# Routing rounds, list scatters and distances between dependent steps in a one-core scan and mixture-of-experts kernel

## What is computed

```python
x = x + layernorm(attn(layernorm(x)))        # x: (4, 1024, 256) f32
x = x + layernorm(ffn(layernorm(x)))

# attn: a state space scan, 16 states for each of 256 channels
xc, z = split(x @ W_in.T)
xs = silu(conv3(xc, conv_w))
dt, B, C = softplus(...), ..., (...) @ W_C.T  # all from xs @ W_x.T
s[t] = exp(-exp(A_log) * dt[t]) * s[t-1] + B[t] * dt[t] * xs[t]
out = (C * s.sum(states) + D * xs) @ W_out.T * silu(z)

# ffn: 8 experts, the best two of each token, and a shared expert
w, sel = top_k(softmax(x @ gate_w.T), 2)      # w made to sum to 1
out = sum_k w_k * (gelu(x @ W1[sel_k] + b1) @ W2[sel_k] + b2)
out = out + gelu(x @ sW1 + sb1) @ sW2 + sb2   # hidden size 1024
```

## Time and profile before

| | us |
|---|---|
| median of 3 runs (lowest, highest) | 1270.08 (1268.75, 1271.2) |
| profiled execution, device time | 1270.0 |
| its span in the trace | 1268.1 |
| TensorE (PE) busy | 1046.6 |
| VectorE (DVE) busy | 711.1 |
| POOL busy | 650.6 |
| ScalarE (ACT) busy | 618.7 |

### The profile page before, as it was taken

The page is one execution under the profiler, slowest core; times in us unless marked ns, Lnnn a source line. Parts: engine busy times, 40 slices in busy tenths (PEclk is TensorE's granted clock), DMA queues, the critical chain, the costliest instruction groups (busy, mean ns, idle before and its releaser), DMA issues. The chain is left out here.

```text
span 1268.1 us, 15496 instructions
## 1 busy us (share of the span) xinstructions
PE 1046.6 (83%) x4738; PEld 836.1 (66%) x4738; DVE 711.1 (56%) x1310; ACT 618.7 (49%) x1186; POOL 650.6 (51%) x695
## 2 busy tenths in 40 slices
PE   4455588678588788697775999999999999999995
PEld 2122266355365565475554788888999999999885
DVE  1699997999797797896897424101010010100585
ACT  3784868666568557587534232222222222233243
POOL 2496967749848569769488335422223222221011
PEclk9675779689589698798887999999999999999998
DMA  4000010100401100713114379449988878784632
GB/s 138 17 9 25 33 34 23 60 1 26 137 1 42 42 10 18 224 42 104 42 28 112 121 235 282 104 144 385 386 270 266 276 253 276 252 280 155 202 114 83
DMA packets 139491, 166.56 MB, mean 131 GB/s; under 512 B 28598, under 2 KB 122383, under 8 KB 139408
## 3 DMA queue, kind: packets, MB, share of 16 engines
q1 hardware_dynamic: 130448, 147.66, 36.4%
q0 software_dynamic: 8960, 17.91, 4.2%
HBM read 141.59 MB, written 24.99 MB: 131 GB/s over the span
## 5 line engine op out<-in xcount | busy, mean ns | idle before, releaser
L1529 POOL TENSOR_TENSOR Ssum<-Ssum,S 128x512 f32<-128x512 f32 x240 | 303.5, 1270 | 45.8 <-DVE S L1139 44.6
L996 PE MATMUL psum<-w,hT 128*128 128x256 f32 x1152 | 258.9, 382 | 2.1 <-issue 2.1
L996 PEld LDWEIGHTS psum<-w,hT 128*128 128x128 f32 x1152 | 218.4, 192 | 35.9 <-issue 7.1
L1421 ACT ACTIVATE A<-dts,nea 128x512 f32<-128x512 f32 x256 | 177.6, 719 | 80.0 <-DVE S L1139 61.3
L963 PE MATMUL psum<-XT,w 128*128 128x256 f32 x800 | 188.7, 393 | 14.5 <-issue 14.5
L1459 ACT ACTIVATE hT<-psum,bb 128x256 f32<-128x256 f32 x200 | 84.0, 471 | 233.9 <-PE psum L963 233.9
L1120 DVE TENSOR_TENSOR psum<-us,psum 128x512 f32<-128x512 f32 x256 | 163.2, 682 | 42.3 <-PE psum L886 40.2
L963 PEld LDWEIGHTS psum<-XT,w 128*128 128x128 f32 x800 | 156.8, 198 | 39.6 <-issue 16.7
L1565 POOL DMA_INDIRECT z_d<-y,ID x72 | 72.3, 1005 | 211.3 <-DVE y L1267 199.0
L886 PE MATMUL psum<-bst,SEL 96*128 96x512 bf16 x128 | 56.5, 443 | 127.9 <-DVE S L1139 113.0
L1139 DVE TENSOR_TENSOR_SCAN S<-A,carry,psum 128x512 f32<-128x512 f32 x120 | 149.1, 1266 | 0.0
(11 more groups left out here) (154 smaller groups left out, 1349.3 us busy)
## 6 DMA issues: line engine op xcount, KB each, us to landing
w<-W SPq DMA_DIRECT2D x94, 1024.0 KB, 5.9
Z<-z_d SPq DMA_DIRECT2D x32, 256.0 KB, 6.3
bb<-b SPq DMA_DIRECT2D x47, 128.0 KB, 7.3
xnb<-x SPq DMA_DIRECT2D x16, 256.0 KB, 3.1
Xr<-x SPq DMA_DIRECT2D x16, 256.0 KB, 5.1
x_d<-gb SPq DMA_DIRECT2D x8, 512.0 KB, 3.0
xn_d<-nb SPq DMA_DIRECT2D x8, 512.0 KB, 3.6
X<-x_d SPq DMA_DIRECT2D x16, 256.0 KB, 7.6
```

The source lines that it names most:

```text
L996: t = eng.matmul(bank(g)[:, 256 * k:256 * k + 256], hT[n % 2][:, f, 128 * k:128 * k + 128], w[:, f, :], start=f == 0, stop=f == 7)
L1421: eng.activation(A[m % NA], dts[i % 2][:, c, :], ACT.Exp, scale=nea[:, c, n:n + 1]).then_inc(decay, 1)
L1529: eng.tensor_tensor(to, to, of, ALU.add).then_inc(nsum, 1)
```

## The change

- Rounds end behind chunks 2, 4, 6 and 7 (counted from 0) instead of 1, 3, 5 and 7: they have 12, 8, 8 and 4 token tiles.
- Beside the scans, two scatters of a list take three steps instead of two.
- There is one more step between `silu` and `dtc`, between `softplus` and `dt_sum`, between `top2` and `soft`, behind a `turn`, and between Gelu and `down`.
- `post` is laid over scans 0 to 27 instead of 29.
- Beside the scans a feed-forward step waits until at most two banks are in use (three before).
- The feed-forward gets 26 steps in 32 scans until the first list is there, and 42 afterwards, instead of 32.
- There are two output buffers `y` instead of three.

```diff
-NR = NC // 2
-TILES = [-(-(4 * TC * (r + 1) - E * 255) // 256) for r in range(NR)]
+ROUND_END = [3, 5, 7, 8]
+NR = len(ROUND_END)
+ROUND = [range(4 * a, 4 * b) for a, b in zip([0] + ROUND_END, ROUND_END)]
+TILES = [-(-(2 * TC * n - E * 255) // 256) for n in ROUND_END]
...
-NY = 3
-FIRST_POST, LAST_POST, FIRST_PREP, LAST_PREP = 0, 29, 0, 25
+NY = 2
+FIRST_POST, LAST_POST, FIRST_PREP, LAST_PREP = 0, 27, 0, 25
...
-    def room(n):
-
-        while len(open_uses) > room_for[0] - n:
+    def room():
+
+        while len(open_uses) > room_for[0] - (2 if past[0] else 3):
             yield
...
         say("silu", i)
         yield
         yield
+        yield
...
         say("low_out", i)
+        yield
         yield
...
     def route(r):
-        while 2 * r + 1 not in posted:
+        while ROUND_END[r] - 1 not in posted:
             yield
         yield
         say("top2", r)
         yield
+        if not past[0]:
+            yield
         say("soft", r)
...
-        for n in range(16):
+        for n in range(2 * len(ROUND[r])):
             say("table", r, n)
...
-            if r < NR - 1 or n % 2:
+            if not past[0]:
+                yield
+            if n % 2:
                 yield
...
                     yield from turn(taken[0] - 1)
+                    yield
                     yield
...
-            for _ in range(3):
+            for _ in range(4):
                 yield
             for n in two:
                 yield from down(n, False)
...
             if i:
-                part(beside, 1)
+
+                calls = 42 if listed[0] else 26
+                part(beside, calls * (k + 1) // 32 - calls * k // 32)
...
+    past[0] = True
     say("widen")
```

More of the change, by code:

```diff
@@ L303, in up @@
         for u in range(4):
-            yield from room(2)
+            yield from room()
             g = next(use)
@@ L372, in pairs @@
                 return
-    ended, summed = [False], set()
+    ended, past, summed = [False], [False], set()
     def direct():
@@ L675, in build @@
         ID = put("ID", [128, 2 * NT + NHALF, 2], i32)
[L676 to L681, removed]
+        R = put("R", [128, 4 * 8 * WIDE])
+        pr, oh1, oh2, eq = (R[:, 8 * WIDE * i:8 * WIDE * (i + 1)].rearrange("p (j e) -> p j e", e=8) for i in range(4))
+        pos, ge = pr, R[:, 8 * WIDE:8 * WIDE + 8 * MOST].rearrange("p (k e) -> p k e", e=8)
+        M = put("M", [128, WIDE + 1, 8])
+        mx, m2, ix, dd = (put(f"q{i}", [128, WIDE]) for i in range(4))
+        posf = put("posf", [128, 2 * WIDE])
         fi = put("fi", [128, 8], i32)
@@ L925, in _ @@
                     ps = take(g)
[L927 to L931, removed]
+                    w = len(ROUND[r])
+                    eng.wait_ge(top, TOP * (r + 1))
+                    eng.matmul(ps[:, 0:8 * w + 8], tri, M[:, 0:w + 1, :].rearrange("p j e -> p (j e)"),
+                               start=True, stop=False)
+                    for j in range(w):
+                        t = eng.matmul(ps[:, 8 * j + 8:8 * w + 8], ones, M[:, j:j + 1, :].to_broadcast([128, w - j, 8]),
+                                       start=False, stop=j == w - 1)
                     t.then_inc(full[BANK[g]], 1)
@@ L1175, in _ @@
                     r, = a
-                    eng.wait_ge(lg_out, 2 * r + 2)
+                    tiles = ROUND[r]
+                    w, logits = len(tiles), lg[:, tiles.start:tiles.stop, :]
+                    eng.wait_ge(lg_out, ROUND_END[r])
                     if r:
                         eng.wait_ge(soft, r)
[L1179 to L1185, removed]
-                    one(top, eng.tensor_tensor(dd, m2, mx, ALU.subtract))
-                    assert done[top] == TOP * (r + 1) + 1
+                    one(top, eng.memset(M[:, w, :], 0.0))
+                    best(logits, mx, oh1[:, 0:w, :], w)
+                    one(top, eng.scalar_tensor_tensor(pr[:, 0:w, :], oh1[:, 0:w, :], -3e38, logits, ALU.mult, ALU.add))
+                    best(pr[:, 0:w, :], m2, oh2[:, 0:w, :], w)
+                    one(top, eng.tensor_tensor(M[:, 0:w, :], oh1[:, 0:w, :], oh2[:, 0:w, :], ALU.add))
+                    one(top, eng.tensor_tensor(dd[:, 0:w], m2[:, 0:w], mx[:, 0:w], ALU.subtract))
+                    assert done[top] == TOP * (r + 1)
                 elif step == "weigh":
                     r, = a
-                    sl = slice(8 * r, 8 * r + 8)
+                    w, sl = len(ROUND[r]), slice(ROUND[r].start, ROUND[r].stop)
                     eng.wait_ge(soft, r + 1)
-                    one(weigh, eng.tensor_scalar(mx, dd, 1.0, None, ALU.add))
-                    one(weigh, eng.reciprocal(wts[:, 0, sl], mx))
-                    one(weigh, eng.tensor_tensor(wts[:, 1, sl], dd, wts[:, 0, sl], ALU.mult))
+                    one(weigh, eng.tensor_scalar(mx[:, 0:w], dd[:, 0:w], 1.0, None, ALU.add))
+                    one(weigh, eng.reciprocal(wts[:, 0, sl], mx[:, 0:w]))
+                    one(weigh, eng.tensor_tensor(wts[:, 1, sl], dd[:, 0:w], wts[:, 0, sl], ALU.mult))
                     assert done[weigh] == WEIGH * (r + 1)
@@ L1434, in _ @@
                     r, = a
[L1435 to L1436 removed]
+                    w = len(ROUND[r])
+                    eng.wait_ge(top, TOP * (r + 1))
+                    eng.activation(dd[:, 0:w], dd[:, 0:w], ACT.Exp).then_inc(soft, 1)
                 elif step == "up_out":
```

51 lines of the change are left out of this document (27 added, 24 removed).

## The result

| | kernel before | changed kernel |
|---|---|---|
| median of 20 runs each (lowest, highest), us | 1270.87 (1268.7, 1273.23) | 1264.66 (1260.45, 1270.96) |
| ratio, 95% interval | | 0.9952, 0.9939 to 0.9966 |
| span of the profiled execution | 1268.1 | 1262.1 |
| scan k = 27 of chunk 7 ends ("the point") | 694.7 | 687.5 (forecast 649) |
| from the point to the end | 573.4 | 574.6 (forecast 564) |

A forecast was written before the change was run, and what follows sets the result against it. VectorE's chain of scans was taken to bound the kernel up to the point, TensorE's leftover matmuls behind it. Terms of -45.8 us before and -9.5 us behind gave -55.3 us, from 1270.0 to 1215 us, range 1196 to 1244.

The forecast's parts named there:

- The two stages: Up to scan k = 27 of chunk 7 VectorE's chain of scans sets the end; behind it TensorE's remaining matmuls do.
- rival of a falling clock: TensorE's clock falls to its lower level in chunks 5 to 7: slower, 1298 us at 0.65; chance 0.04.
- (g): POOL in chunk 4: 22 list scatters beside its other work make 82 us, so POOL paces that chunk: +9 us.
- (h): TensorE in chunk 6: 42 steps on 32 scans, 28 feed-forward parts instead of 19, 85 us of work: +8 us.
- (b): VectorE's waits behind list scatters on POOL, and stretched `nm`, go away: -19.1 us; sign: L1484 waits under 4 us.
- (c): One more step between silu and `dtc` removes TensorE waits that delay `spread`: -11 us, bounds nothing and 18.1.
- (d): One more step from softplus to `dt_sum` gives -8, fewer banks in use before an `up` -4.7: -12.7 us.
- -4.7 for the banks: With at most two banks in use before an `up`, TensorE's waits for the bank `dt_sum` empties no longer delay `spread`.
- (e): Fewer feed-forward parts between two spreads, 26 steps on 32 scans in chunks 2 to 4: -7 us, bounds 0 and 8.6.
- (a): One routing round fewer on VectorE before the point, 10.5 us less 0.8 for larger rounds: -9.7 us.
- (j): TensorE behind the point: one tile group fewer left, -14.3, less added work; list loads and scatters hidden: -9.5 us.
- Chunks 4 to 7 have no room left: Rival: POOL and TensorE are near VectorE there, so removed waits turn up elsewhere: 1240 us; chance 0.22.

The follow-up runs named there:

- f13: Changed kernel with the carry copies of even chunks on ScalarE instead of POOL: 1268.36 us, 0.9949 of the kernel before.
- e6: Changed kernel plus a 128x384 memset on POOL at every second scan from chunk 3 on: chunks 3 to 7 longer by 0.0, 4.1, 4.4, 2.1, 0.2 us.
- f12: Changed kernel with rounds ending behind chunks 1, 3, 5, 7 again, 32 feed-forward steps in chunks 4 to 6 and 64 in chunk 7: 1248.05 us, ratio 0.9785.
- e5: Changed kernel with 32 feed-forward steps instead of 42 once a list is there, 26 before that: one run, chunk 6 92.5 us, rest behind the point 603.1 us.
- f15: The changed kernel unaltered, run again as the measure for other runs: 1270.79 us, 0.9958 of the kernel before.
- e9: Changed kernel with 32 feed-forward steps in chunks 4 to 6 once a list is there and 64 in chunk 7: 1257.2 us, ratio 0.9905.
- e2: As e1, with the thinning of list scatters taken back as well, so scatters stand at every scan: 1285.91 us, ratio 1.0125.
- e1: Changed kernel with rounds ending behind chunks 1, 3, 5 and 7 again, all else kept: 1272.23 us, ratio 1.001.
- e10: Changed kernel without the one step more behind silu and the one behind softplus: 1262.9 us, ratio 0.9939.
- f16: As f12, without the one step more behind silu and the one behind softplus: 1252.1 us, ratio 0.9818.
- e3: Changed kernel with 32 feed-forward steps on 32 scans throughout instead of 26 and then 42: 1275.5 us, ratio 1.0042.
- VectorE's probe: Changed kernel plus a 128x384 memset on VectorE at every second scan from chunk 3 on: chunks 3 to 7 longer by 1.5, 1.2, 6.0, 1.5, 1.9 us.
- e4: Changed kernel with post laid over scans 0 to 29 again instead of 27: 1260.75 us, ratio 0.9924.
- f17: As f12, with 80 feed-forward steps instead of 64 in chunk 7: 1259.3 us, ratio 0.9866.

## Why the prediction was wrong, step by step

**What was right.** The two stages and the point between them; that waits for `spread` would fall (forecast to some 22 us, measured 17.1); that chunks 2 and 7 would get shorter (by 7.2 and 12.9 us); no clock below 0.8 in chunks 4 to 7 (0.80 to 0.88), so that the rival of a falling clock didn't occur. Of the signs named for being wrong, the late point came: 687.5 us, where 670 was the limit.

**(g) is the step that failed first.** It took POOL's work in chunk 4 as a sum, 82 us, and made that the chunk's length. The work was 77.3 us, below forecast, and the chunk took 95.4. A sum gives a chunk's length only if the engine can work ahead, and POOL can't: in the first third, where VectorE has no pause, it waits for scans (5.2 us at 348.8) and for ScalarE (4.4 us at 366.3); in the last 60 us, where the residual, convolution, `u` and 15 scatters meet, it is busy 57.4. VectorE then waits 6.6 us for `gb`, 3.0 for a power and 6.8 for the carries. I had seen POOL's columns but not asked which of its results are wanted at once. f13 and e6 show POOL's hand in chunk 4; f12 shows what comes of taking the scatters out: 86.2 us with more TensorE work. This step and the next left chunks 4 and 6 13 and 18 us above their forecasts of 82 and 83, of 38.5 us by which the point came too late.

**(h) was mis-sized.** Forecast for 42 steps: chunk 6 at 83 us, +8. Measured by e5 against f15: 8.5 us in chunk 6, but 3.6 more in chunk 5, and some 7 in chunk 7 (65.4 against 58.8), 19 in all. And with 32 steps chunk 6 already takes 92.5 us, where the forecast had taken VectorE's 75 for the floor. The 42 steps buy two groups of the end stage rather than the one that the sum had, and behind the point f15 is 21.1 us shorter than e5. So they about break even; the work pays in chunk 7 (e9). Why chunk 6 takes 92.5 us with 32 steps is not taken apart; VectorE waits 14.4 us there, 6.1 of them for a carry copy.

**(b) in kind right, moved elsewhere.** `nm` waits 11.4 us where it waited 13.4, now in chunks 4 and 6. The sign named for it, under 4 us, failed. The forecast took the scatters' price for a matter of density. Thinning is worth 13.7 us in odd chunks (e2 against e1), which (b) put at 19.1 for both parts.

**(c), (d): the two steps of distance, forecast -19, measured 0** (e10), and some -4 in f12's surroundings (f16). The -4.7 for the banks was not tested by itself. Waits for the softplus were 9.1 us and are 9.5, of which 7.7 lie in one place of chunk 6, where 32 steps leave 3.2 (e5). The error was to take stalls singly from the earlier trace rows and to add them up: e10 loses in chunks 0 and 1 and gains in the crowded chunks. That other waits of the same chunk had covered these stalls is my reading; no run takes a single one away.

**(e) was too low for its chunks:** 26 early steps instead of 32 are worth 12.3 us in chunks 2 and 3 (e3), forecast 7. But chunk 4, where the change still makes 26, is 4.5 us shorter with 32; why was not tested, and it brings the sum near the forecast.

**(a)** A round fewer is there, but VectorE's busy time up to the point fell only from 569.7 to 566.6 us. Part of the rest is stretched operations (below); what remains was not taken apart. f12 has the round more and isn't slower up to the point than e9: what the round costs there, taking the scatters out of the even chunks gives back. The two were not separated.

**(j): forecast -9.5, measured +1.2.** TensorE was busy 549.3 us there, 6.6 less than before (forecast 9.5), and idle 7.8 us more. Of that, one gap of 6.55 us stands ahead of 869.5, where it waits for weights:

```profile
833.84 3.81 SPq L1662 DMA_DIRECT2D ID<-list_d  x4
838.47 24.41 SPq L1664 DMA_DIRECT2D ID<-list_d  x22
863.70 0.38 SPq L1680 DMA_DIRECT2D w<-W  x1
...
869.48 3.71 PE L978 MATMUL psum<-XT,w 128*128 128x256 f32 x9 [6.55 <-DMA bb<-b]
```

The 26 loads of the last list's numbers occupy SyncE for 28.2 us, and the weights' fetches stand behind them. I had counted eight list loads and called them hidden. The kernel before has the same 22 loads (24.2 us from 817.9), 20 us earlier, and TensorE doesn't wait there. Nor does it wait in f15, the same program, where SyncE is as long at it but TensorE is late already; that execution has 582 us from the point to the end (below).

**The rivals.** "Chunks 4 to 7 have no room left" was right in kind and its 1240 us too low by 25: it took the same sum for chunk 4, with 12 us instead of 9. It had 0.22 where the forecast had 0.52.

**What stays open.** Why VectorE's probe costs all of itself in chunk 5 (its wait for the logits there grows from 4.6 to 7.6 us, which is half of it); why chunk 4 is shorter with 32 steps than with 26; what else holds chunk 6; and how much of (a) was lost to what.

## What to carry to other kernels

Busy time summed over a stretch bounds it from below only. In chunk 4 VectorE was busy 34.4 of the first 35.2 us and POOL 57.4 of the last 60.2: the bounds of the parts add up, though neither engine's sum comes near the whole. Where engines hand results to and fro, ask of each added instruction in an in-order queue which wanted result stands behind it, and put it where nothing is wanted soon: here 21 scatters beside carry copies made chunk 4 9 us longer than it is without them (e9, f12). Stalls that lie in the same stretch aren't additive; a probe of a few us of idle work on one engine tells in one run whether that engine paces a stretch. Work begun ahead of a point isn't gained until its matmuls are done ahead of it: count them on both sides (e4, f17). And the parts of a change can't be judged one by one: thinning and 26 early steps gained, but the new round ends gain 0.6% beside 42 steps and lose 1.2% beside 32 and 64.

## What the runs showed of the hardware

**Stretched small operations of VectorE came back.** VectorE and POOL, chunk 5:

```profile
472.53 3.66 DVE L1099 TENSOR_SCALAR rs<-mv,C 128x4 f32<-128x4 f32 x1
```
```profile
471.25 4.91 POOL L1547 TENSOR_TENSOR Ssum<-Ssum,S 128x512 f32<-128x512 f32 x4
```

Four elements a partition take 3.66 us, where the same operation took 0.23 at 429.5 us, and end as POOL's four sums end (476.2 us). Two more, of 128x8 and 128x64, took 2.84 (L1207, 514.2 us) and 2.49 us (L1057, 687.8), and each ends with a pair of sums. The Trainium skill, "SBUF — State Buffer", section "SBUF: two separate sides", says that a GpSimd operation and a VectorE operation in a two-port mode, or with two SBUF inputs against a GpSimd operation that reads SBUF, take a shared port pair as an exclusive lock, each for the whole instruction. The rows agree that one engine waits for the other. They show more than one instruction waited for: the 3.66 us reach over three of the four sums. And L1099 and L1207 read one tile, with constants; no row shows in which mode they run. `nm` behind the long wait at 582.8 us took 0.16 us now, and the stretching stands where POOL next has a run of sums, as the prediction had feared.

**The granted clock behind the point differs between executions of one kernel.** Sums from the point to 800 us, of the change and of f15, the same program:

```profile
687.50:800.00 112.50, 107.38 (x517) 92.56 (x517) 41.20 (x118) 37.15 (x72) 45.14 (x45) 0.98 0.64 169
```
```profile
687.70:800.00 112.30, 100.40 (x458) 84.58 (x457) 36.98 (x100) 30.83 (x61) 45.29 (x45) 0.94 0.63 170
```

The second got through 59 matmuls fewer in the same time, and its span is 7.6 us longer, with chunks equal within 1.1 us. From 769 to 779 us its TensorE had pauses of up to 1.8 us, 6.8 us in all, in which it waited for nothing that the profile shows, and the granted clock was at its lower level for a part of them (0.73 in the mean); the change had no pause and 1.00. F15 in these 10 us, then the change:

```profile
769.00:779.00 10.00, 3.21 (x10) 1.90 (x9) 0.08 (x1) 1.17 (x3) 5.61 (x6) 0.73 1.07 171
```
```profile
769.00:779.00 10.00, 10.00 (x49) 8.84 (x48) 1.44 (x3) 1.48 (x4) 7.56 (x9) 1.00 0.98 166
```

What makes these pauses is open. The changed kernel's 20 runs spread over 10 us, those of the kernel before over 4.5; its three slowest have mean clocks of 0.889 to 0.891, its three fastest 0.895 and 0.896. A difference of a few us behind the point in a single profile is therefore no finding.
